# Short attentions in a vision-transformer tower: one stationary query tile for both head halves, keys masked per half

## The reference

```python
qkv = x @ w_qkv.T                       # 192 -> 3 x 192 (the first one adds a bias)
q, k, v = 12 heads of 16 channels each
scores = q @ k.T * scale                # per head, 37 x 37
# NEIGH:  scale*(1.2 q.k) - 0.2*scale*(q3 . k3), q3/k3 = sums over three neighbouring tokens (band)
# CAUSAL: scores masked where key > query
# DIAG:   scores masked where key == query
out = softmax(scores) @ v
```

## Time and profile before

| | |
|---|---|
| median of 3 runs | 1878.59 us (1874.66 to 1887.67) |
| the profiled execution | 1880.07 us, its span 1878.3 us |
| mean granted TensorE clock | 0.851 |
| PE matmul busy | 1609.9 us (86%), 11941 records |
| PE weight load busy | 1493.8 us (80%) |
| DVE busy | 1067.8 us (57%) |
| ACT busy | 812.7 us (43%) |
| POOL busy | 512.2 us (27%) |
| chain that ended last | PE 54%, issue 22%, DVE 16%, ACT 4% |

### The profile page before, as it was taken

The page is one execution under the profiler, slowest core; times in us unless marked ns, Lnnn a source line. Parts: engine busy times, 40 slices in busy tenths (PEclk is TensorE's granted clock), DMA queues, the critical chain, the costliest instruction groups (busy, mean ns, idle before and its releaser), DMA issues.

```text
span 1878.3 us, 33999 instructions
## 1 busy us (share of the span) xinstructions
PE 1609.9 (86%) x11941; PEld 1493.8 (80%) x11941; DVE 1067.8 (57%) x2975; ACT 812.7 (43%) x1979; POOL 512.2 (27%) x1259
## 2 busy tenths in 40 slices
PE   5898995984988998899977999788989999789980
PEld 5787874984877898889977999688878898779970
DVE  4665555332654777457765444367755778634437
ACT  2453531432555554345433555344543544245520
POOL 3255244004432121522232000453126123300031
PEclk8765855995557999999889999879989989899995
DMA  5020001551088000100004676300011000167731
GB/s 154 26 78 28 25 21 54 149 161 27 24 269 249 2 1 18 47 18 1 16 16 133 202 224 216 96 15 2 1 48 34 1 11 20 29 191 229 224 94 35
DMA packets 87756, 149.78 MB, mean 80 GB/s; under 512 B 7380, under 2 KB 58883, under 8 KB 87590
## 3 DMA queue, kind: packets, MB, share of 16 engines
q1 hardware_dynamic: 81254, 135.35, 23.6%
q0 software_dynamic: 6336, 12.26, 2.3%
HBM read 106.59 MB, written 41.05 MB: 79 GB/s over the span
## 4 chain that ended last, share of the span: by engine, by line
PE 54%; issue 22%; DVE 16%; ACT 4%; POOL 2%; DMA 2%; DVEq 0%; POOLq 0%; SPq 0%; ACTq 0%
PE ps_proj L1065 10%; PE ps_proj L1188 6%; PE ps_score L1259 5%; PE ps_proj L1079 5%; PE ps_proj L1242 4%; PE ps_o L1160 4%; PE ps_pt L1030 4%; PE ps_score L1116 4%; PE ps_o L1150 3%; PE ps_score L1127 2%; DVE prob L1593 2%; DVE prob L1590 2%; DVE negmax L1592 2%; PE ps_proj L1046 1%; PE ps_turn L1008 1%
## 5 line engine op out<-in xcount | busy, mean ns | idle before, releaser
L1259 PE MATMUL ps_score<-w,hid 128*112 128x192 f32 (+2 forms) x1680 | 300.2, 330 | 6.9 <-DVE x L1902 6.9
L1259 PEld LDWEIGHTS ps_score<-w,hid 128*112 128x112 f32 (+2 forms) x1680 | 272.8, 177 | 8.9 <-DVE x L1902 8.7
L1383 ACT ACTIVATE hid<-ps_proj 128x224 f32<-128x224 f32 (+2 forms) x360 | 137.8, 385 | 267.7 <-PE ps_proj L1242 267.7
L1490 POOL TENSOR_SCALAR tmp<-rs,var 111x1 f32<-111x1 f32 x110 | 40.5, 368 | 607.2 <-DVE rs L1561 606.8
L1448 POOL DMA_INDIRECT tin<-rows_out,idx x66 | 67.3, 1019 | 467.1 <-issue 363.8
L1030 PE MATMUL ps_pt<-const,prob 111*111 111x111 f32 x660 | 126.7, 310 | 36.7 <-ACT probt L1371 24.8
L1188 PE MATMUL ps_proj<-wo,ot 128*111 128x192 f32 (+1 forms) x616 | 141.5, 380 | 3.9 <-ACT ot L1349 3.7
L1030 PEld LDWEIGHTS ps_pt<-const,prob 111*111 111x111 f32 x660 | 94.8, 202 | 56.8 <-issue 23.7
L1371 ACT ACTIVATE probt<-ps_pt 111x333 f32<-111x333 f32 x176 | 78.8, 448 | 127.1 <-PE ps_pt L1030 126.6
L1160 PEld LDWEIGHTS ps_o<-v,probt 111*111 111x111 f32 x1056 | 126.1, 191 | 0.4
L1188 PEld LDWEIGHTS ps_proj<-wo,ot 128*111 128x111 f32 (+1 forms) x616 | 113.8, 206 | 15.5 <-issue 12.8
(11 more groups left out here) (256 smaller groups left out, 4212.2 us busy)
## 6 DMA issues: line engine op xcount, KB each, us to landing
w_in<-w_all_dram SPq DMA_DIRECT2D x130, 384.0 KB, 3.5
w<-w_all_dram SPq DMA_DIRECT2D x50, 576.0 KB, 5.2
rows_in<-zero SPq DMA_DIRECT2D x1, 12320.0 KB, 46.1
rows_out<-zero SPq DMA_DIRECT2D x1, 9240.0 KB, 79.9
tin<-rows_in SPq DMA_DIRECT2D x36, 224.0 KB
rows_out<-tout SPq DMA_DIRECT2D x36, 168.0 KB
patch<-patches_dram SPq DMA_DIRECT2D x11, 333.0 KB, 3.0
wo<-wo_all_dram SPq DMA_DIRECT2D x6, 576.0 KB, 3.9
```

Of the source, the lines that this page charges most:

```text
L1259: last = pe.matmul(bank[0:n, 0:C], hid[:, i % 2, m, at:at + n], w2[:, slot, m, :], start=(m == 0), stop=(m == FC - 1))
L1383: act.activation(hid[:, i % 2, m, 0:n], bank[:, 0:n], ACT.Relu if b.tile is None else ACT.Gelu).then_inc(taken, 1)
```

## The change

Scores: one matmul per chunk and image instead of one per half. The stationary tile is the whole query tile (112 rows, both halves), and the moving operand is 2 x 37 columns: the image's keys with the second half's rows zeroed, and with the first half's rows zeroed. A group's 444 score columns lie in one PSUM bank, so the groups alternate between two banks, and there is one mask matmul of 444 columns. For that the keys are stored twice, each copy scaled by a 0/1 column per row (`half`): in CAUSAL and DIAG the eviction of a key projection becomes two ACT instructions; in NEIGH a new ACT step `KS b part` of four instructions makes the masked keys, `part` 0 from the plain keys and `part` 1 from their sums. `S` in NEIGH waits for `ks_ready` in place of `band_done`.

Storage: NEIGH's plain queries and keys and the key sums become single-buffered and lie in `wo` and `relbias`, which are not yet needed; the loads of `relbias` and `wo` move from the start to the step PV(9) of NEIGH on SP's queue, and the addition of the block mask to `relbias` goes away (the host stores it so).

V's bias: one fp32r matmul of 33 rows, two of them not zero, in place of the fp32 one; DVE makes its operands in the set-up (six small instructions).

```diff
-            ("QK", 0, 2), ("QK", 0, 3), ("QS", 0, 0, 0), ("QS", 0, 0, 1), ("BD", 0, 1), ("NX", 3), ("TOK", 6),
-            ("V", 0, 0), ("QS", 0, 1, 0), ("QS", 0, 1, 1), ("NX", 4), ("NX", 5)]
+            ("QK", 0, 2), ("QK", 0, 3), ("QS", 0, 0, 0), ("QS", 0, 0, 1), ("KS", 0, 0), ("BD", 0, 1), ("NX", 3), ("TOK", 6),
+            ("V", 0, 0), ("QS", 0, 1, 0), ("QS", 0, 1, 1), ("KS", 0, 1), ("NX", 4), ("NX", 5)]
...
-NEIGH_QS = {(1, 1): [(0, 0)], (1, 2): [(0, 1)], (2, 0): [(1, 0)], (2, 1): [(1, 1)]}
+NEIGH_MASKED = {(1, 1): [("QS", 0, 0)], (1, 2): [("QS", 0, 1), ("KS", 0)], (2, 0): [("QS", 1, 0)],
+                (2, 1): [("QS", 1, 1)], (2, 2): [("KS", 1)]}
...
-            for dst, src in ((row[:], rows), (gatew[:], gates_w), (relbias[:], bias_src)):
+            for dst, src in ((row[:], rows), (gatew[:], gates_w)):
                 load_const(dst, src, late_in)
-            load_wo(CAUSAL)
...
+                    if step[1] == 9:
+                        sp.wait_ge(ks_ready, 2 * NB)
+                        load_const(relbias[:], bias_src, bias_in)
+                        sp.wait_ge(qs_ready, 4 * NB)
+                        load_wo(CAUSAL)
...
-                        last = pe.matmul(bank[0:TG, 0:C], const[0:1, K_ONES:K_ONES + TG], early[0:1, Y_VB:Y_VB + C],
-                                         start=False, stop=True)
+                        last = pe.matmul(bank[0:TG, 0:C], two_ones[:], vbias[:], start=False, stop=True)
...
                             pe.wait_ge(qs_ready, 4 * (b + 1))
-                            pe.wait_ge(band_done, 2 * (b + 1))
+                            pe.wait_ge(ks_ready, 2 * (b + 1))
...
-                        for bank in banks:
-                            if a != NEIGH:
-                                pe.matmul(bank[0:TG, 0:2 * TG], identb[:],
-                                          maskb[:, a, 0:2, :].rearrange("p h k -> p (h k)"),
-                                          start=True, stop=False, skip_group_check=True)
+                        bank = banks[0][0:TG, 0:4 * TG]
+                        if a != NEIGH:
+                            pe.matmul(bank, identb[:], maskb[:, a, :, :].rearrange("p h k -> p (h k)"),
+                                      start=True, stop=False, skip_group_check=True)
...
                         for j in range(2):
                             for i in range(IPG):
+                                t, col = t0 + i * NTOK, (j * IPG + i) * 2 * NTOK
                                 for part, (q_t, k_t) in enumerate(parts):
-                                    for e, bank in enumerate(banks):
-                                        at, col = 64 * e, (j * IPG + i) * NTOK
-                                        ins = pe.matmul(bank[0:TG, col:col + NTOK],
-                                                        q_t[at:at + 64, j, g - s.blocks[b][0], i, :],
-                                                        k_t[at:at + 64, j, t0 + i * NTOK:t0 + (i + 1) * NTOK],
-                                                        start=(a == NEIGH and part == 0),
-                                                        stop=(part == len(parts) - 1), skip_group_check=True)
+                                    ins = pe.matmul(bank[:, col:col + 2 * NTOK], q_t[0:TL, j, g - s.blocks[b][0], i, :],
+                                                    k_t(b % 2, j)[0:TL, :, t:t + NTOK], start=(a == NEIGH and part == 0),
+                                                    stop=(part == len(parts) - 1), skip_group_check=True)
...
                     elif j >= 2:
-                        act.activation(short_k(b % 2)[:, j - 2, 0:n], bank[:, 0:n], ACT.Copy).then_inc(taken, 1)
+                        for e in range(2):
+                            ins = act.activation(short_k(b % 2, j - 2)[:, e, 0:n], bank[:, 0:n], ACT.Copy,
+                                                 scale=half[:, e:e + 1])
+                        ins.then_inc(taken, 1)
...
+                elif kind == "KS":
+                    _, b, part = step
+                    if part:
+                        act.wait_ge(band_done, 2 * b + 2)
...
+                    for j in range(2):
+                        for e in range(2):
+                            ins = act.activation(real((neigh_kb if part else short_k)(b % 2, j)[0:TL, e, 0:n]),
+                                                 by_group((plain_kb if part else plain_k)[:, j, 0:n // TP * TG]),
+                                                 ACT.Copy, scale=half[0:TL, e:e + 1])
+                    ins.then_inc(ks_ready, 1)
...
-                _, taken, value = take_score((st, "S", g, 0, 1))
-                scores = ps_score[0:TG, :, 0:2 * TG].rearrange("p e (s k) -> p e s k", k=NTOK)
+                bank, taken, value = take_score((st, "S", g, 0, 0))
+                scores = bank[0:TG, 0:4 * TG].rearrange("p (s e k) -> p s e k", e=2, k=NTOK)
```

More of the change, by code:

```diff
@@ L517, in numbered @@
         elif step[0] == "S":
-            for e in range(2):
+            for e in range(1 if ATTS[st[1]].short else 2):
                 score[(*key, e)] = len(score)
@@ L784, in short_q, with short_k, neigh_kb, real @@
             return flat[:, 0:2 * 3 * IPG * HWIDE].rearrange("p (j g i m) -> p j g i m", j=2, g=3, i=IPG)
[L786 to L796, removed]
+        def short_k(slot, j):
+            return qk[:, slot, 6 + 2 * j:8 + 2 * j, :]
+        def neigh_kb(slot, j):
+            return kb_rest[:, slot, :, :] if j else qk[:, slot, 10:12, :]
+        plain = relbias[:].rearrange("p h k -> p (h k)").rearrange("p (w j n) -> p w j n", w=2, j=2)
+        plain_k, plain_kb = plain[:, 0], plain[:, 1]
+        plain_q = wo[:, 0:2 * 3 * TG].rearrange("p (j n) -> p j n", j=2)
+        def real(rows_of):
+            return rows_of.rearrange("p (a t) -> p a t", t=TP)[:, :, 0:TG]
+        def by_group(rows_of):
+            return rows_of.rearrange("p (a t) -> p a t", t=TG)
+        half = hscale[:, 28:30]
         scales = hscale[:, 0:24].rearrange("p (a j h) -> p a j h", a=4, j=2)
@@ L1035, in att_step @@
                 s = ATTS[a]
[L1036 removed]
+                if step[0] in ("NX", "BD", "QS", "KS", "XA", "LATE", "W1", "LD", "ND"):
                     return
@@ L1088, in att_step @@
                     p = step[2]
-                    banks = [score_bank((*key, e)) for e in range(2)]
+                    banks = [score_bank((*key, e)) for e in range(1 if s.short else 2)]
                     b = s.block_of[g]
@@ L1311, in _ @@
                     if a == NEIGH:
-                        dst = neigh_q(b % 2)[:, j, 0:n] if j < 2 else short_k(b % 2)[:, j - 2, 0:n]
-                        act.activation(dst, bank[:, 0:n], ACT.Identity, bias=hscale[:, 24 + j:25 + j]).then_inc(taken, 1)
+                        if b:
+                            act.wait_ge(band_done, 2 * b - 1 if j < 2 else 2 * b)
+                            act.wait_ge(qs_ready, 4 * b)
+                            act.wait_ge(ks_ready, 2 * b)
+                        rows = 128 if j < 2 else TL
+                        dst = plain_q[:, j, 0:n // TP * TG] if j < 2 else plain_k[:, j - 2, 0:n // TP * TG]
+                        act.activation(by_group(dst), real(bank[0:rows, 0:n]), ACT.Identity,
+                                       bias=hscale[0:rows, 24 + j:25 + j]).then_inc(taken, 1)
                     elif a >= T5:
@@ L1682, in band @@
                 dve.wait_ge(proj_taken[n % 2], n // 2 + 1)
-                if b and not which:
-                    dve.wait_ge(qs_ready, 4 * b)
-                src, dst = [t.rearrange("p j n -> p (j n)").rearrange("p (a t) -> p a t", t=TP)[:, :, 0:TG]
-                            .rearrange("p a (i q) -> p a i q", i=IPG)
-                            for t in ((short_k(b % 2), neigh_kb(b % 2)) if which else (neigh_q(b % 2), qb[:]))]
+                if b:
+                    dve.wait_ge(*((ks_ready, 2 * b) if which else (qs_ready, 4 * b)))
+                src, dst = [t.rearrange("p j n -> p (j n)").rearrange("p (a q) -> p a q", q=NTOK)
+                            for t in ((plain_k, plain_kb) if which else (plain_q, qb[:]))]
                 end = NTOK - 1
-                link(dve.tensor_copy(dst[:, :, :, 0:1], src[:, :, :, 0:1]))
-                link(dve.tensor_tensor(dst[:, :, :, 1:], src[:, :, :, 1:], src[:, :, :, 0:end], ALU.add))
-                tell(dve.tensor_tensor(dst[:, :, :, 0:end], dst[:, :, :, 0:end], src[:, :, :, 1:], ALU.add), band_done,
+                link(dve.tensor_copy(dst[:, :, 0:1], src[:, :, 0:1]))
+                link(dve.tensor_tensor(dst[:, :, 1:], src[:, :, 1:], src[:, :, 0:end], ALU.add))
+                tell(dve.tensor_tensor(dst[:, :, 0:end], dst[:, :, 0:end], src[:, :, 1:], ALU.add), band_done,
                      2 * b + which + 1)
@@ L1758, in _ @@
                         link(dve.memset(v64[:, :, :, T5_D:T5_D + 1], 1.0))
+                    if step[1:] == (0, 0) and st[1] == T5:
```

(3 more changed lines are left out.)

67 lines of the change are left out of this document (40 added, 27 removed).

## The result

The changed kernel takes 1900.4 us (median of 20 runs, 1882.4 to 1906.0) beside 1888.1 us for the kernel before on the same chip (20 runs, 1874.0 to 1895.9). The ratio is 1.0057, with a 95% interval of 1.0037 to 1.0077: **10.8 us slower**, where 5 us faster was forecast. Runs in a slower state of the chip, among them one of 7859 us of the version with stalls, are left out of the comparisons.

The account below looks back on a forecast made before the run. PE was taken as the bound on paper, half its speed withheld by the clock. Terms -2.4 - 4.9 + 3.7 + 12.5 + 2.6 = +11.5, with -16.5 for the clock, gave -5 us: 1874 us, range 1848 to 1894.

Parts of the forecast that it names:

- The score stream: Scores of the three short attentions: full-array instructions at 97 to 101 ns replace half-array pairs at 97 ns; 0 us.
- load not overlapped: Rival, scores: each full-array load and its stream run one after the other; +48 us, 1922 us, chance 0.02.
- stream halved: Rival, scores: the 74 moving columns set the pace, not the load; -24 us, 1850 us, chance 0.04.
- ACT's waits: Added ACT work delays PE: +3.7 before NEIGH's first scores, +12.5 at blocks 1 to 3, +2.6 for CAUSAL and DIAG keys.
- Lead: Before NEIGH's first scores, 44 to 51 us: KS 0 0 and KS 0 1 stand in ACT's line, +3.7 us.
- V's bias: NEIGH: one matmul priced at its load saves 0.4 or 0.7 us on ten groups, -5.6; with mode changes, -4.9 counted.
- CAUSAL and DIAG: Their scores: fewer changes between half-array and full-array instructions, -2.4 us; extra key evictions on ACT, +2.6 us.
- 13 lost exits: CAUSAL and DIAG: in 13 of 22 groups, 37-row transposes after the scores newly pay a tiling-mode change, +3.4 us.
- The clock: NEIGH and DIAG: full-array scores make clock falls rarer; -10 for two NEIGH groups, -6.5 in DIAG, -16.5 us together.
- no clock gain: Rival: clock falls need a wait of PE too, and the change adds waits; +5 to +18, about 1889 us, chance 0.20.
- Slower by KS: Rival, NEIGH: blocks begin behind 3 us waits, scores start at half clock; about +26, 1905 us, chance 0.07.
- three signs of being wrong: Scores' pace unlike L1160's, ACT's masked copies far from 0.46 us, or the three stages' clock moving by more than 0.15.

Follow-up runs that it names:

- the version with stalls: Changed kernel without its KS steps (NEIGH's masked keys zeros), PE made to wait for a 16-byte transfer ahead of groups 3, 6 and 9: 0.9978 of before.
- without KS: Changed kernel without its eight KS steps, NEIGH's masked keys being zeros written once at the start: 0.9891 and, the second time, 0.9908 of before.
- KS alone: Kernel before plus the eight ACT copies per block, written to an unread spare buffer, with the scores waiting for them: 1.0132 of before, 25 us more.
- the bias alone: Kernel before with only NEIGH's V bias changed to one fp32r pass over two rows: 0.9947 of before, 10 us less.

## Why the prediction was wrong

**The score stream: right.** Forecast 97 to 101 ns per full-array load and 186 at half clock; 97 and 186 were read. 74 moving columns hide behind their load, as L1160's 65 did: at half clock they take 186 ns a load, and the logits with 8 moving columns took 180 to 190. Halving the instructions brought nothing. Both rivals on the stream (load not overlapped, stream halved) are out.

**ACT's waits: right within 1 us.** Lead +3.7 forecast, 3.8 read; three block waits 8.4, 8.8 read; KS b 0 ahead of the turned probabilities 4.1, and 4.5 to 5.0 read; keys in DIAG 2.2 of the 2.6, and the wait for them went from 3.1 to 5.8 us.

**V's bias: too small, and its own price too high.** Forecast -4.9 with the mode changes of NEIGH; alone it measured -10 (-4 to -16) by the times and -7 by NEIGH's length. The pass was priced at its load, 0.10 or 0.19 us, and took 0.28 at full clock (79.26 in the chain of the changed kernel) and 0.42 at half (68.63): 3.5 us saved on the ten groups, not 5.6. The stage gained more than that, at a slightly higher clock in its traces, which the term did not have.

**CAUSAL and DIAG: close without the clock.** -2.4 and +2.6 were forecast, -1 (-7 to +5) measured. One piece is mis-added: 13 lost exits at +3.4 are 0.26 us each, more than any of its prices for a change (0.12 to 0.24); at the 0.2 of the entries they are +2.6. But -6.5 of clock in DIAG was in the sum, and half a microsecond is what the traces show of it, less than their scatter.

**The clock: the step that failed.** The prediction took -16.5. Its larger part, -10 for two NEIGH groups out of five, exists: without KS NEIGH is 9.9 us shorter than with half-array scores. What failed is adding it to +12.5 of waits as if the two were independent. The text named the danger ("behind which the clock can fall as it did at 108") and gave it no price in the sum, only 5 us a group in a rival. The runs show the price: KS's 13.3 us of waits in NEIGH cost 24, and 5.8 us of bare stalls cost 17.5. So the gain was made and given back in the same stage. In place of -16.5 the sum should have had nothing or less; +11.5, its sum without the clock, lies 0.7 from the measured 10.8. The agreement is partly luck: the bias is 5 better than priced, and KS alone costs 25, not the 16.2 of lead and blocks. The three parts measured alone (-10, -1, +25) add up to 14; with their intervals of 6 to 8 us either way, they leave no gain to be seen for NEIGH's full-array scores once KS stands ahead of them. The rival "no clock gain" (+5 to +18, chance 0.20) is what happened. "Slower by KS" described the mechanism (stall, scores at half clock), but without the gain beside it, and put 26 us on it; the run with KS alone, on the old scores, came out at 25.

**What would show it.** The signs all came: the pace, the first scores at 56 us, waits of 3 us at groups 3, 6 and 9, clocks above 0.67 and 0.58. None of the three signs of being wrong came. They were the signs of terms, and two were badly chosen. NEIGH's mean clock rose from 0.68 to 0.71 while its length grew, because the bias alone brings 0.72. And the first scores start at 51.1 us in the trace before, but at 54.2 to 56.7 in the nine other traces without a KS step: their time scatters by more than the +3.7, and only the wait in front of them, 8.1 us for 4.3, tells the lead.

## What to carry to other kernels

Price a clock gain together with the waits that the same change makes: here stalls of 2 to 3 us of PE ahead of a block of work cost NEIGH two to three times their length (18.2 us for 8.8, 17.5 for 5.8), and a gain of 10 us was there only without them. When a mask or a layout is needed in a copy, make it where the data is written already (an eviction split by rows) and not in a step of its own on an in-order engine that feeds the bound; the step's place in the queue decides more than its work. And before a full-array form is hoped to be faster than two half-array ones, look at the pace of the loads: if loads set it, only a side effect, here the clock, is left.

## What the hardware showed

- Two half-array loads of 111 fp32 columns took 97 ns a pair, and one full-array load of as many took 97 ns: the halves load side by side. At half clock the full-array load took 186.
- A full-array load of 111 fp32 columns hid the stream of 74 moving ones of the matmul before it, on the same rows. The Trainium skill, "TensorE: Matmul & The Clock Gate", Part 3, says in its list of what overlaps that this comes only when the row group differs. The trace disagrees: at half clock the logits with 8 moving columns had 180 to 190 ns a load, the scores with 74 had 186 (128.31 to 129.05), so 66 more moving columns cost nothing.
- The granted clock stayed at 1.00 through a stall of 1.73 us and fell within the 3.55 us of scores behind it; in a stall of 2.93 us it fell before the stall ended. Without a stall the same scores ran at 1.00 throughout.
- With the same bias pass, NEIGH ran at 0.72 with half-array scores and at 0.80 to 0.84 with full-array ones, where no stall was added, in five traces; with stalls at 0.70 to 0.72, in four.
